# Values products of two key blocks back to back, query and key halves staged for three products, and a new order table, in an MLP, attention, MLP kernel

## The chip, the cores and the metric

One Trainium2 chip, one core. The metric is the device time of one execution in microseconds. PE is the matrix engine, PEld its weight load, ACT the scalar engine, DVE the vector engine, POOL GpSimd, SP the queue that starts transfers.

## The reference

Four sequences of 2048 rows of 256 numbers. Three residual layers follow one another: half an MLP, attention, half an MLP.

```python
x = x + 0.5 * ffn(layernorm(x));  x = x + attn(layernorm(x));  x = x + 0.5 * ffn(layernorm(x))
# ffn: input, hidden and weights rounded in blocks of 16 to a scaled grid of 8 magnitudes
h = silu(xq @ wgate_q.T) * (xq @ wup_q.T); y = quant(h) @ wdown_q.T          # 256 -> 704 -> 256
# attn: 8 heads, each a difference of two softmaxes over queries and keys of 16 numbers
q, k = rotary(rmsnorm(x @ Wq.T)), rotary(rmsnorm(x @ Wk.T)); v = x @ Wv.T    # 16 maps of 16, 8 values of 32
a = softmax(causal(q @ k.T / 4)); out = (a[first] - lam * a[second]) @ v
y = (layernorm(out) * (1 - LAMBDA_INIT)) @ Wproj.T
```

## The kernel before

The rows are cut into 64 tiles of 128; four tiles are a chunk, four chunks a sequence, so there are 16 chunks. A chunk goes through the first MLP (pass 0), the projections of attention (pass 1), attention itself, the output projection (pass 2) and the second MLP (pass 3). Different chunks are in different stages at a time, and the five engines each run one fixed list of work, joined by semaphores.

Attention goes in steps (`attention_steps`, L108): a step is one chunk of 512 queries, one group `g` of two heads (four score maps) and one block of 128 keys. There are 640 steps. A chunk with number 0, 1, 2, 3 in its sequence has 4, 8, 12, 16 key blocks for each of the four groups; in the last four blocks, on the diagonal, only 512, 384, 256 or 128 queries are left. A step is:

- `scores` twice (`u` 0 and 1, L1541 to L1553): PE multiplies a stack of key parts and a stack of query parts, 64 rows each, two products side by side in two halves of the array (its tiling is 64x128), into `psum_s0` or `psum_s1`. `scores(s, u)` waits until `exp(s-1, u)` has read that tile.
- `exp` twice (L1243): ACT reads a `psum_s` tile, 1024 numbers a row, and writes `probs`, a ring of three steps.
- `mask` (L1152): POOL, on diagonal blocks only.
- `values` (L1556 to L1571): PE multiplies four float32 probabilities with v, in four column strips (tiling 128x32), and adds them up in `psum_o`. The trace has each of the four float32 products as two instructions. It waits for its own step's exp or mask.

All other products on PE (`hidden` L1514, `down` L1527, `project_qk` and `project_v` L1538, `transpose_o` L1578, `project_out` L1588) use the whole array, 128x128, and are called fills here. So PE changes its tiling between scores, values and fills.

Queries and keys are kept as the float16 part and the float16 rest. `high_qk` (ACT, L1233) writes the float16 part of a tile twice into the four slots of `st_q` and of `st_k`, and `low_qk` (POOL, L1134 to L1143) writes the rest, float32 minus float16 part, twice, in one instruction for queries and one for keys. Slots are query: part, part, rest, rest; key: part, rest, part, rest; so a score is the sum of four products of halves. `turn_qk` (SP, L1062) turns both stacks by transposing transfers.

The order of each engine's list is made at build time. `whole_plan` (L253) adds stages with an engine, a weight from `COST` (L89), a due time and what they need, take and free; `Plan.order` (L161) then places one stage after another, the one that can start first, and among equals the one due first. Due times come from the table `DUE` (L61): spans, offsets and shifts for the chunks, and one nudge for each kind of stage. `SWITCH` (L105) is what the planner counts for a change of tiling.

Of the kernel before, what the change touches and what calls it, by code (L numbers as in the profile page):

```python
# [14 lines left out]
P = 128  # L15
# [40 lines left out]
EARLY = BATCHES * NCH  # L56

DUE = dict(lead=12, spans=(21, 703, 35, 11832, 953, 6799, 105, 2598, 104, 4129, 21, 1789, 27, 50, 55, 14564), tail=566708347155116, early=-0.41, mlp1=(149, 28), qkv=(41, 70), qk=(-35, 167), out=(-1336, 93), mlp2=(373, 152), shift=((-18, -8, -25, -3, 0), (-234, 83, 0, -6, 13), (-20, -9, -45, -17, 0), (-21, -3, -20, 2, 194), (13, 6, 1, 24, -5), (0, -15, -31, 3, 13), (-57, 0, 172, 14, 3), (-16, -29, -15, -10, 0), (59, 22, 6, 22, 13), (-6, -27, 4, -8, 1), (-10, -94, 16, 2, -6), (-3, 8, -3, -7, -16), (-12, -71, -111, 3, -54), (12, -3, -25, -41, -80), (-3, 10, 47, -15, -6), (21, 0, 0, 7, 0)),  # L61
           nudge=dict(add_down=-58, add_out=13, copy_xT=-55, dequant_h=35, dequant_x=-14,
                      divide_h=21, divide_x=1, down=3, gate=-26, grid_h=-3, grid_x=10, head_stats=4,
                      heads_out=-8, hidden=20, high_h=-6, high_x=11, load=-1, low_h=-2, low_qk=4,
                      low_x=-28, mask=-1, norm_a=149, norm_heads=-2, norm_qk=30, norm_x=52,
                      points_h=10, points_x=4, project_out=1, project_qk=-2, project_v=-2,
                      quant_h=6, quant_x=87, read_qk=-37, read_v=56, rms=45, rope=10, rope_add=-3,
                      scale_x=-10, scores=-517, stats=23, store=-7, tanh=5, transpose_o=15,
                      transpose_x=-26, turn_qk=13, turn_x=10, values=-6))
ST = 2  # L70
LANDING = 4.0
# [5 lines left out]

# [11 lines left out]
COST = dict(add_down=0.46, add_out=0.47, copy_o=0.67, dequant_h=1.38, dequant_x=1.06, divide_h=1.39,  # L89
            divide_x=1.06, down=1.97, gate=0.82, grid_h=0.89, grid_x=0.68, head_stats=2.75, heads_out=3.15,  # L90
            hidden=1.29, high_h=0.8, high_qk=1.16, high_x=0.64, low_h=1.52, low_qk=2.28, low_x=1.16,
            mask=0.63, norm_a=1.09, norm_heads=0.69, norm_qk=0.68, norm_x=0.78, points_h=0.89, points_x=0.69,
            project_out=0.69, project_qk=1.36, project_v=0.69, quant_h=1.65, quant_x=2.06, read_qk=0.69,
            read_v=0.48, rms=4.05, rope=1.93, rope_add=1.27, rstd=3.34, scale_x=1.29, square_h=0.79,
            square_x=0.62, stats=1.82, tanh=0.46, transpose_o=0.59)
OVERLAP = dict(tensor=0.0, vector=0.08, scalar=0.1, gpsimd=0.04, sync=0.0)
REACH = dict(tensor=0.14, vector=0.04, scalar=0.04, gpsimd=0.08, sync=0.1)
RELEASE = 0.06
DRAIN = 0.14
TILING = dict(scores=1, values=2)  # L100

PORT = dict(grid_h=0, points_h=0, norm_qk=0, norm_heads=0, norm_x=0, quant_x=0.81,
            divide_x=0, dequant_x=0, low_x=0, divide_h=0, dequant_h=0, low_h=0, rope_add=0, low_qk=0, mask=0)
PORT_LEAD = 0.14
SWITCH = 0.11  # L105
# [18 lines left out]
def by_act(key):  # L124

    pas, p = key
    return pas != 2 and 2 * p // NTC < EARLY


# [11 lines left out]
class Plan:  # L141

    def __init__(self, nudge):
        self.nudge = nudge
        self.stages = {}
        self.sizes = {}  # L150
        self.ring = {}
        self.bank = {}

    def add(self, name, engine, weight, due, needs=(), takes=(), frees=(), lands=0.0):
        weight = COST.get(name[0], weight)
        if engine == "tensor":
            lands += DRAIN
        self.stages[name] = (engine, weight, due + self.nudge.get(name[0], 0),
                             [n for n in needs if n], list(takes), list(frees), lands)

    def order(self):  # L161
        end, free_at = {}, dict.fromkeys(ENGINES, 0.0)
        freed = {r: {} for r in self.sizes}
        self.ring = {r: {} for r in self.sizes}
        banks = [[0.0, 0] for _ in range(BANKS)]
        out = {e: [] for e in ENGINES}
        tiling, left = 0, {}
        held = {"vector": 0.0, "gpsimd": 0.0, "part": 0.0}
# [7 lines left out]
        met = {name: 0.0 for name in self.stages if not missing[name]}  # L176
# [21 lines left out]
        while len(end) < len(self.stages):  # L198
            best = None
            for name in met:  # L200
                at = ready(name)
                if at is not None:
                    start = max(at, free_at[self.stages[name][0]])
                    if self.stages[name][0] == "tensor" and TILING.get(name[0], 0) != tiling:
                        start += SWITCH
                    if best is None or (round(start, 6), place[name]) < best[:2]:
                        best = (round(start, 6), place[name], start, name)
            assert best, "stages that wait for one another: " + str(list(met)[:20])
            start, name = best[2:]
# [9 lines left out]
            if name[0] in PORT and engine in held:  # L219
# [5 lines left out]
                extra = max(0.0, until - start - PORT_LEAD)  # L225
                held[engine] = start + extra + lock
                if engine == "gpsimd":
                    held["part"] = start + extra + (lock / 2 if name[0] == "low_qk" else lock)
# [17 lines left out]
        self.end = end  # L246
        return out
# [5 lines left out]
def whole_plan():  # L253
# [3 lines left out]
    plan = Plan(DUE["nudge"])  # L257
# [6 lines left out]
    def fill(name, weight, due, needs, takes=(), frees=()):  # L264

        add(name, "tensor", weight, due, needs, [("bank", name), *takes], frees)

    def halved(pas, p, due, made):

        u = ("x", pas, p)  # L270
        add(("high_x", *u), "scalar", .65, due, [made], [(rings_of(pas)[1], (pas, p))])
        add(("low_x", *u), "gpsimd", 1.35, due + .7, [("high_x", *u)], [], [(rings_of(pas)[0], (pas, p))])
        add(("turn_x", *u), "sync", .2, due + 2, [("low_x", *u)], [(rings_of(pas)[2], (pas, p))], [(rings_of(pas)[1], (pas, p))],
            lands=3.3)

    def quantise(kind, key, due, needs, takes, frees, times):

        quant, divide, square, grid, points, dequant, high, low, lands = times
        own, half, turned = (("xu", "x16", "xT16") if kind == "x" else ("hu", "h16", "hT16"))
        u = (kind, *key)  # L280
        q = ("quant_" + kind, *u)
        if kind == "x" and by_act(key):
            norm, q = ("norm_a", *u), ("scale_x", *u)
            add(norm, "scalar", .8, due, needs, takes, frees)
            add(q, "vector", 1.3, due, [norm], [("bank", q)], [("bank", q)])
        else:
            add(q, "vector", quant, due, needs, [*takes, ("bank", q)], [*frees, ("bank", q)])
        add(("divide_" + kind, *u), "gpsimd", divide, due + .1, [q])
        sq = ("square_" + kind, *u)
        place = ("gu", u) if kind == "h" else ("bank", sq)  # L290
        add(sq, "scalar", square, due + .2, [("divide_" + kind, *u)], [place])
        add(("grid_" + kind, *u), "vector", grid, due + .3, [("square_" + kind, *u)])
        add(("points_" + kind, *u), "vector", points, due + .4, [("grid_" + kind, *u)], [],
            [place] if kind == "x" else [])
        add(("dequant_" + kind, *u), "gpsimd", dequant, due + .5, [("points_" + kind, *u)], [], [place] if kind == "h" else [])
        add(("high_" + kind, *u), "scalar", high, due + .6, [("dequant_" + kind, *u)], [(half, key)])
        add(("low_" + kind, *u), "gpsimd", low, due + .7, [("high_" + kind, *u)], [], [(own, key)])
        add(("turn_" + kind, *u), "sync", .2, due + .8, [("low_" + kind, *u)], [(turned, key)], [(half, key)],
            lands=lands)

    def mlp(pas, tiles, due, pace, stats):
        for i in range(0, NTC, 2):
            d = due + pace * i
            pair = (pas, tiles[i] // 2)
            quantise("x", pair, d, [("rstd", *stats)], [("xu", pair)], [("stats", stats)] if i else [],
                     (2.3, 1.1, .7, .75, .75, 1.1, .65, 1.35, 3.3))
            for t in tiles[i:i + 2]:
                key = (pas, t)
                dt = d + 6 + pace * (t % 2)
                for part in range(len(PARTS)):  # L310
                    h = ("hidden", pas, t, part)
                    d1 = dt + 2 * part
                    fill(h, 1.3, d1, [("turn_x", "x", *pair), ("hidden", pas, t, part - 1) if part else
                                      ("hidden", pas, t - 1, len(PARTS) - 1) if t % 2 else None], [("hu", key)],
                         [("xT16", pair)] if part == len(PARTS) - 1 and t % 2 else [])
                    add(("tanh", *h), "scalar", .42, d1 + 1.6, [h])
                    add(("gate", *h[1:]), "vector", .9, d1 + 2, [("tanh", *h)], [], [("bank", h)])
                quantise("h", key, dt + 7, [("gate", pas, t, part) for part in range(len(PARTS))], [], [],
                         (1.6, 1.45, .85, 1.0, 1.0, 1.45, .8, 1.75, 4.2))
                dn = ("down", pas, t)  # L320
                fill(dn, 2.1, dt + 13, [("turn_h", "h", *key)], [], [("hT16", key)])
# [11 lines left out]
    for c in chunks:  # L333
        at.append(at[-1] + due["spans"][c])
# [1288 lines left out]
```

## Time and profile before

| what | value |
|---|---|
| runs | 2249.22, 2256.57 and 2260.17 us, median 2256.57 |
| the profiled execution, span from first to last instruction | 2257.2 us |
| its busy time | PE 1906.5, ACT 1724.0, DVE 1677.2, POOL 1438.6 us |
| its mean granted PE clock | 0.962 of full speed |

The page gives the profiled execution's span and no other time of it; the span is 0.6 us above the median of the runs. Busy times are sums over the execution and the engines work side by side, so none of them adds up to the span.

### The profile page before, as it was taken

How to read it: one execution, taken by the hardware profiler on the slowest of the kernel's cores; microseconds unless marked ns; L12 is line 12 of the kernel's file. 1: busy time of each engine (PE TensorE's matmuls, PEld its weight loads, DVE VectorE, ACT ScalarE, POOL GpSimd, SP SyncE). 2: the span in 40 equal slices, each digit the busy share in tenths (PEclk: the TensorE clock that was granted, in tenths of full speed). 3: DMA queues.
4: the chain of work that ended last, by engine and by line, in shares of the span. 5: the costliest groups of instructions: out<-in, count | busy, mean ns of one | idle time of the engine just before them, and what ended most of it. 6: DMA issues, size and time to landing. Idle time of an engine off the chain costs nothing. (4 is left out here: it accounts for less than half of the span.)

```text
span 2257.2 us, 39699 instructions
## 1 busy us (share of the span) xinstructions
PE 1906.5 (84%) x13634; PEld 776.0 (34%) x13634; DVE 1677.2 (74%) x3657; ACT 1724.0 (76%) x2598; POOL 1438.6 (64%) x1490
## 2 busy tenths in 40 slices
PE   2577889989989888999989888998998899988845
PEld 1233333333423333343333332343332433432312
DVE  8898988778837897878856897878864978834324
ACT  3446888878887887878888888887888799788842
POOL 3778886767735787766845786667763868723213
PEclk9789999999999999999999999999999999999977
DMA  4134444235212444233412334233231434211102
GB/s 110 27 64 85 72 76 76 50 62 89 42 45 38 71 71 90 59 54 76 75 45 38 73 67 88 45 75 61 52 63 40 81 63 86 52 39 20 35 10 45
DMA packets 477494, 136.19 MB, mean 60 GB/s; under 512 B 458222, under 2 KB 477038, under 8 KB 477294
## 3 DMA queue, kind: packets, MB, share of 16 engines
q1 hardware_dynamic: 477294, 133.65, 31.6%
q8 instruction: 110, 1.80, 0.3%
q14 instruction: 90, 0.74, 0.1%
HBM read 11.96 MB, written 8.39 MB: 9 GB/s over the span
## 5 line engine op out<-in xcount | busy, mean ns | idle before, releaser
L1243 ACT ACTIVATE probs<-psum_s 128x1024 f32<-128x1024 f32 (+3 forms) x1280 | 1072.9, 902 | 109.8 <-PE psum_s L1553 97.9
L1571 PE MATMUL psum_o<-probs,v_sb 128*32 128x512 f32 (+3 forms) x5120 | 581.8, 542 | 27.6 <-POOL probs L1152 14.7
L1514 PE MATMUL shared<-w_gu_T,xT 128*128 128x480 f16 (+1 forms) x2304 | 510.1, 369 | 84.6 <-DMA xT<-x 49.2
L1553 PE MATMUL psum_s<-q_stack,k_stack 64*128 64x512 f16 (+3 forms) x2560 | 390.8, 353 | 101.2 <-ACT probs L1243 91.6
L1514 PEld LDWEIGHTS shared<-w_gu_T,xT 128*128 128x128 f16 x2304 | 212.4, 99 | 371.6 <-issue 102.1
L1527 PE MATMUL shared<-w_down_T,hT 128*128 128x256 f16 x2176 | 272.7, 282 | 36.1 <-DMA hT<-h 16.4
L1166 ACT ACTIVATE hq<-shared,tanh_scale 128x240 f32<-128x240 f32 (+1 forms) x384 | 172.2, 458 | 133.1 <-PE shared L1514 128.2
L1152 POOL TENSOR_SCALAR_AFFINE_SELECT probs<-probs 128x512 f32<-128x512 f32 x256 | 181.3, 715 | 141.3 <-ACT probs L1243 140.0
L1553 PEld LDWEIGHTS psum_s<-q_stack,k_stack 64*128 64x128 f16 x2560 | 94.9, 93 | 508.3 <-ACT probs L1243 409.9
L1120 POOL TENSOR_TENSOR hq<-grid,qscale 128x704 f32<-128x704 f32 x128 | 182.6, 1428 | 112.6 <-DVE grid L1367 112.6
L1083 POOL TENSOR_TENSOR hq<-hq,rscale 128x704 f32<-128x704 f32 x128 | 186.1, 1455 | 104.0 <-DVE rscale L1277 103.8
L1527 PEld LDWEIGHTS shared<-w_down_T,hT 128*128 128x128 f16 x2176 | 210.9, 101 | 109.0 <-issue 35.5
L1127 POOL TENSOR_TENSOR h<-hq,h 128x704 f16<-128x704 f32 x128 | 201.9, 1578 | 63.3 <-ACT h L1204 63.3
L1127 POOL TENSOR_TENSOR x<-xq,x 128x512 f16<-128x512 f32 x128 | 158.6, 1243 | 95.8 <-ACT x L1204 95.7
L1571 PEld LDWEIGHTS psum_o<-probs,v_sb 128*32 128x32 f32 x5120 | 111.4, 108 | 268.1 <-issue 164.2
L1362 DVE SCALAR_TENSOR_TENSOR hq<-grid,hq 128x704 f32<-128x704 f32 x128 | 149.7, 1170 | 58.5 <-ACT grid L1177 58.1
L1348 DVE SCALAR_TENSOR_TENSOR hq<-hq,shared 128x240 f32<-128x240 f32 (+1 forms) x384 | 147.0, 383 | 58.7 <-ACT hq L1166 57.8
L1538 PE MATMUL shared<-w_qkv_T,xT 128*128 128x512 f16 (+1 forms) x768 | 146.0, 338 | 26.3 <-DVE xb L1374 6.2
L1367 DVE SCALAR_TENSOR_TENSOR grid<-grid,hq 128x704 f32<-128x704 f32 x128 | 160.9, 1257 | 3.3
L1350 DVE SCALAR_TENSOR_TENSOR hq<-hq,shared 128x240 f32<-128x240 f32 (+1 forms) x384 | 153.0, 398 | 13.2
L1190 ACT ACTIVATE xq<-xb,offset,rstd 128x256 f32<-128x256 f32 x192 | 103.5, 599 | 49.9 <-POOL offset L1111 40.6
L1177 ACT ACTIVATE grid<-hq 128x704 f32<-128x704 f32 x128 | 102.0, 797 | 47.4 <-POOL hq L1083 47.2
(133 smaller groups left out, 2372.8 us busy)
## 6 DMA issues: line engine op xcount, KB each, us to landing
xb<-L_attn_x SPq DMA_DIRECT2D x16, 512.0 KB, 4.1
out<-xb SPq DMA_DIRECT2D x16, 512.0 KB, 2.9
xT<-x SPq DMA_TRANSPOSE x128, 3.1
hT<-h SPq DMA_TRANSPOSE x128, 3.5
k_stack<-st_k SPq DMA_TRANSPOSE x64, 3.3
q_stack<-st_q SPq DMA_TRANSPOSE x64, 3.3
k_stack<-L_ffn_w_down SPq DMA_DIRECT2D x1, 704.0 KB, 4.2
k_stack<-L_ffn_w_gate SPq DMA_DIRECT2D x1, 480.0 KB, 6.0
```

Source lines behind the costliest of these rows:

```text
L1083: nc.gpsimd.tensor_tensor(by_block(a), by_block(a), rscale[:, i, 0:nb].unsqueeze(2).broadcast_to([P, nb, QB]), ALU.mult).then_inc(scaled_r ...
L1120: nc.gpsimd.tensor_tensor(by_block(a), by_block(g), qscale[:, i, 0:nb].unsqueeze(2).broadcast_to([P, nb, QB]), ALU.mult).then_inc(quantise ...
L1127: nc.gpsimd.tensor_tensor(low, buffers(kind, key)[0], high, ALU.subtract)\
L1152: nc.gpsimd.affine_select(out=blk, in_=blk, compare_op=ALU.is_ge, fill=0.0, base=0, pattern=[[0, 4], [1, P]], channel_multiplier=-1)\
L1166: nc.scalar.activation(buffers("h", h[1:3])[0][:, lo:hi], bank(h)[:, 0:hi - lo], ACT.Tanh, scale=tanh_scale[:, 0:1]).then_inc(tanh_done, 1)
L1243: nc.scalar.activation(probs[:, s % 3, 2 * u:2 * u + 2, q0:CHUNK], psum_s[u][:, :, q0:CHUNK], ACT.Exp, scale=HD ** -0.5 / QK_SCALE ** 2).t ...
L1350: nc.vector.scalar_tensor_tensor(h2, h2, H_SCALE, bank(h)[:, n:2 * n], ALU.mult, ALU.mult)\
L1367: nc.vector.scalar_tensor_tensor(points(e[1], e[2:]), g, GRID_BASE, a, ALU.add, ALU.subtract)\
L1514: last = nc.tensor.matmul(bank(e)[:, 0:2 * (hi - lo)], xs[:, x, t % 2, k, :], w_gu_T[:, w, k, 2 * lo:2 * hi], start=n == 0, stop=n == len( ...
L1527: last = nc.tensor.matmul(bank(e)[:, 0:C], hs[0:n, k, :], w_down_T[0:n, w, :], start=i == 0, stop=i == len(parts) - 1)
L1553: last = nc.tensor.matmul(psum_s[u][:, j, q0:CHUNK], k_stack[half, at, h, kt % NTC * P:(kt % NTC + 1) * P], q_stack[half, c % 2, h, q0:CHU ...
L1571: last = nc.tensor.matmul(psum_o[at:at + VD, q0:CHUNK], v_sb[:, kt // NTC % SLOTS * NTC + kt % NTC, 2 * g + u, :], probs[:, s % 3, 2 * u + ...
```

## The change

1. **Values in pairs.** In the plan, the values stage of an even key block `k` also needs the exp (or mask) of the next block. The two values stages of a pair can then follow each other on PE. The instructions and their semaphore waits are as before; only their places in PE's list change.
2. **Three products of halves.** One buffer `st` takes the place of `st_q` and `st_k`. Slots are query: part, part, rest, zero; key: rest, part, part, zero. `low_qk` becomes one instruction for queries and keys together that writes 512 numbers a row, where there were two of 512. The fourth slot is zeroed once at the start. The product of the two rests is left out. Score products, transfers and `high_qk` keep their sizes.
3. **Order.** `DUE` becomes a table of due times of each kind of stage, pass (or head group) and chunk, first and last, in integer nanoseconds; `LANDING` and `COST` are the same figures in nanoseconds, but `low_qk` is 1160 where it was 2.28 us. Paths that no stage took (`quant_x`, `norm_x`) are removed. The mask's semaphore count follows POOL's own order.

```diff
-DUE = dict(lead=12, spans=(21, 703, 35, 11832, 953, 6799, 105, 2598, 104, 4129, 21, 1789, 27, 50, 55, 14564), ...
+DUE = {
+    "add_down0": (94794, 240540, 58015, 44956, 84367, 91045, 158882, 108668, 804012, 943216, ...
...
+    def add(self, name, engine, at, needs=(), takes=(), frees=(), lands=0, weight=None):
+
+        family, c, i, n = at
+        first, last = DUE[family][2 * c:2 * c + 2]
+        weight = COST[name[0]] if weight is None else weight
...
-            add(("values", s), "tensor", .90 * w, d, [("mask", s) if diag is not None else ("exp", s, 1),
-                                                      ("values", s - 1) if s else None, ("read_v", tiles[-1])],
-                [("psum_o", (c, g))], [("probs", s)])
+            paired = s + (k + 1) % 2
+            add(("values", s), "tensor", at("values"), [("mask", s) if diag is not None else ("exp", s, 1),
+                                                        ("mask", paired) if steps[paired][5] is not None else ("exp", paired, 1),
+                                                        ("values", s - 1) if s else None, ("read_v", tiles[-1])],
+                [("psum_o", (c, g))], [("probs", s)], weight=900 * full // CHUNK)
...
-        st_q = sb("st_q", [P, ST, 2 * NH, 4, HD], F16)
-        st_k = sb("st_k", [P, ST, 2 * NH, 4, HD], F16)
+        st = sb("st", [P, ST, 2, 2 * NH, 4, HD], F16)
...
+                    nc.gpsimd.memset(st[:, :, :, :, 3, :], 0.0).then_inc(fills_done, 1)
...
-                            for j, (stage, hi, lo) in enumerate(((st_q, slice(0, 2), slice(2, 4)),
-                                                              (st_k, slice(0, 4, 2), slice(1, 4, 2)))):
-                                pool.wait_ge(hi_ready, 2 * t + j + 1)
-                                st = stage[:, t % ST]
-                                src = roped[:, t % NTC, j * C:(j + 1) * C].rearrange("p (h d) -> p h d", d=HD)
-                                nc.gpsimd.tensor_tensor(st[:, :, lo, :],
-                                                        src.unsqueeze(2).broadcast_to([P, 2 * NH, 2, HD]),
-                                                        st[:, :, hi, :], ALU.subtract).then_inc(lo_ready, 1)
+                            pool.wait_ge(hi_ready, 2 * t + 2)
...
+                            src = roped[:, t % NTC, :].rearrange("p (j h d) -> p j h d", j=2, d=HD)
+                            nc.gpsimd.tensor_tensor(parts(2 * HD, n - 2 * HD), src, parts(HD, n), ALU.subtract)\
+                                .then_inc(lo_ready, 1)
...
-                                pe.wait_ge(masked, d + 1)
+                                pe.wait_ge(masked, MASK["mask", s] + 1)
```

What the new order does is not seen in the table. Three places show it.

**PE in the middle**, around step 277 of 640 (the eighth chunk), where fills stand between attention steps. L1553 or L1585 are scores, L1571 or L1603 values, the others fills. Before:

```order
L1553 MATMUL psum_s<-q_stack,k_stack 128x512 x4
L1571 MATMUL psum_o<-probs,v_sb 32x512 x4
L1514 MATMUL shared<-w_gu_T,xT 128x480 x12
L1514 MATMUL shared<-w_gu_T,xT 128x448 x6
L1553 MATMUL psum_s<-q_stack,k_stack 128x512 x4
L1571 MATMUL psum_o<-probs,v_sb 32x512 x4
L1514 MATMUL shared<-w_gu_T,xT 128x480 x6
```

Now:

```order
L1585 MATMUL psum_s<-q_stack,k_stack 128x512 x4
L1603 MATMUL psum_o<-probs,v_sb 32x512 x8
L1585 MATMUL psum_s<-q_stack,k_stack 128x512 x4
L1546 MATMUL shared<-w_gu_T,xT 128x480 x12
L1546 MATMUL shared<-w_gu_T,xT 128x448 x6
L1559 MATMUL shared<-w_down_T,hT 128x256 x17
L1585 MATMUL psum_s<-q_stack,k_stack 128x512 x4
L1603 MATMUL psum_o<-probs,v_sb 32x512 x8
```

The values of two steps stand together, and the fills between the scores of two steps.

**PE at the end**, in the last group of the last chunk, where no fill is left. The numbers 0 and 1 of `psum_s` are `u`. Before:

```order
L1553 MATMUL psum_s0<-q_stack,k_stack 128x512 x2
L1553 MATMUL psum_s1<-q_stack,k_stack 128x512 x2
L1571 MATMUL psum_o<-probs,v_sb 32x512 x4
L1553 MATMUL psum_s0<-q_stack,k_stack 128x512 x2
L1553 MATMUL psum_s1<-q_stack,k_stack 128x512 x2
L1571 MATMUL psum_o<-probs,v_sb 32x512 x4
```

Now:

```order
L1585 MATMUL psum_s0<-q_stack,k_stack 128x512 x2
L1585 MATMUL psum_s1<-q_stack,k_stack 128x512 x2
L1585 MATMUL psum_s0<-q_stack,k_stack 128x512 x2
L1585 MATMUL psum_s1<-q_stack,k_stack 128x512 x2
L1603 MATMUL psum_o<-probs,v_sb 32x512 x8
```

Before, one step's values stand between the scores of any two steps; now nothing, and then the values of two.

**POOL**, the first tiles of queries and keys (`st`, `st_q` and `st_k` are the staged halves, `x`, `xq` and `hq` belong to other stages). Before:

```order
L1143 TENSOR_TENSOR st_q<-roped,st_q 128x16x32
L1143 TENSOR_TENSOR st_k<-roped,st_k 128x32x16
L1143 TENSOR_TENSOR st_q<-roped,st_q 128x16x32
L1143 TENSOR_TENSOR st_k<-roped,st_k 128x32x16
L1120 TENSOR_TENSOR xq<-xq,qscale 128x512
```

Now:

```order
L1192 TENSOR_TENSOR x<-xq,x 128x512
L1210 TENSOR_TENSOR st<-roped,st 128x2x16x16 x2
L1192 TENSOR_TENSOR x<-xq,x 128x512
L1152 TENSOR_TENSOR hq<-hq,rscale 128x704 x2
L1210 TENSOR_TENSOR st<-roped,st 128x2x16x16
```

Each tile has one instruction where it had two.

## Rows read from the trace of the kernel before

**Rows 1.** The page, part 1: busy time of each engine.

```profile
PE 1906.5 (84%) x13634; PEld 776.0 (34%) x13634; DVE 1677.2 (74%) x3657; ACT 1724.0 (76%) x2598; POOL 1438.6 (64%) x1490
```

**Rows 2.** Busy time by stretch: PE, PEld, DVE, ACT, POOL, granted clock, DMA share, GB/s.

```profile
200.00:2000.00 1800.00, 1617.53 (x11815) 654.37 (x11815) 1405.34 (x3087) 1476.46 (x2227) 1234.13 (x1269) 0.98 0.35 64
2000.00:2150.00 150.00, 131.81 (x1004) 40.59 (x1006) 55.38 (x126) 131.81 (x164) 39.72 (x44) 1.00 0.11 25
2150.00:2257.00 107.00, 50.70 (x280) 22.32 (x272) 42.43 (x93) 30.79 (x48) 32.07 (x32) 0.70 0.14 29
```

**Rows 3.** Waits of the whole span: engine, line waited for, total us, times, longest.

```profile
ACT probs L1243 <- PE psum_s L1553: 97.9, 125, 4.8
...
PE psum_s L1553 <- ACT probs L1243: 91.6, 179, 1.6
...
PE psum_o L1571 <- POOL probs L1152: 14.7, 30, 1.0
```

**Rows 4.** PE in order of time among fills: start us, length us, then the group.

```profile
829.85 1.39 PE L1514 MATMUL shared<-w_gu_T,xT 128*128 128x480 f16 x6
831.07 1.15 PE L1527 MATMUL shared<-w_down_T,hT 128*128 128x256 f16 x9
...
997.05 1.07 PE L1571 MATMUL psum_o<-probs,v_sb 128*32 128x512 f32 x8
998.05 1.39 PE L1514 MATMUL shared<-w_gu_T,xT 128*128 128x480 f16 x6
999.37 0.61 PE L1553 MATMUL psum_s<-q_stack,k_stack 64*128 64x512 f16 x4
999.90 1.06 PE L1571 MATMUL psum_o<-probs,v_sb 128*32 128x512 f32 x8
```

**Rows 5.** The same for PE, three values steps in a row.

```profile
2105.35 0.39 PE L1553 MATMUL psum_s<-q_stack,k_stack 64*128 64x512 f16 x2 [0.61 <-ACT probs L1243]
2105.67 0.66 PE L1578 MATMUL shared<-ident,o_sb 128*128 128x128 f32 x4
...
2106.58 2.78 PE L1571 MATMUL psum_o<-probs,v_sb 128*32 128x512 f32 x24
2109.30 0.60 PE L1553 MATMUL psum_s<-q_stack,k_stack 64*128 64x512 f16 x4
```

**Rows 6.** The same for PE in the attention-only end.

```profile
2138.41 1.92 PE L1571 MATMUL psum_o<-probs,v_sb 128*32 128x512 f32 x16
2140.27 0.61 PE L1553 MATMUL psum_s<-q_stack,k_stack 64*128 64x512 f16 x4
...
2142.16 1.07 PE L1571 MATMUL psum_o<-probs,v_sb 128*32 128x512 f32 x8
...
2147.79 1.06 PE L1571 MATMUL psum_o<-probs,v_sb 128*32 128x512 f32 x8
```

**Rows 7.** ACT in order of time in the same end.

```profile
2122.78 10.53 ACT L1243 ACTIVATE probs<-psum_s 128x1024 f32<-128x1024 f32 x12 [0.63 <-PE psum_s L1553]
...
2140.76 9.55 ACT L1243 ACTIVATE probs<-psum_s 128x1024 f32<-128x1024 f32 x10 [0.89 <-PE psum_s L1553]
```

**Rows 8.** Groups of POOL, shapes apart: count, busy us, mean ns, idle before.

```profile
L1143 POOL TENSOR_TENSOR st_k<-roped,st_k 128x512 f16<-128x512 f32 x64 | 82.4, 1288 | 0.0
L1143 POOL TENSOR_TENSOR st_q<-roped,st_q 128x512 f16<-128x512 f32 x64 | 81.9, 1279 | 39.6 <-ACT st_q L1233 39.5
...
L697 POOL TENSOR_TENSOR k_stack<-k_stack,hq 128x1536 f32<-128x1536 f32 x3 | 10.2, 3391 | 26.4 <-DVE k_stack L761 26.4
...
L691 POOL MEMSET v_sb<- 128x5120 f32 x1 | 4.4, 4370 | 0.0
```

**Rows 9.** Groups of DVE, shapes apart.

```profile
L1367 DVE SCALAR_TENSOR_TENSOR grid<-grid,hq 128x704 f32<-128x704 f32 x128 | 160.9, 1257 | 3.3
...
L1424 DVE TENSOR_TENSOR roped<-roped,qk_rstd 128x512 f32<-128x512 f32 x64 | 62.2, 1001 | 0.3
...
L1391 DVE TENSOR_TENSOR roped<-shared,rope_sb 128x512 f32<-128x512 f32 x64 | 43.5, 680 | 0.0
```

More of the change, by code:

```diff
@@ L54 @@
 XB = XC * NTC
[L56 to L69, printed above, removed]
@@ L224, in order @@
                     until = held["vector"]
[L225 removed]
+                extra = max(0, until - start - PORT_LEAD)
                 held[engine] = start + extra + lock
                 if engine == "gpsimd":
[L228 removed]
+                    held["part"] = start + extra + (lock // 2 if name[0] == "low_qk" else lock)
                 weight += extra
@@ L246, in order @@
         self.end = end
+        self.left = left
         return out
@@ L296, in quantise @@
[L296 to L301, printed above, removed]
+        add(("dequant_" + kind, *u), "gpsimd", at("dequant_" + kind), [("points_" + kind, *u)], [], [place] if kind == "h" else [])
@@ L307, in mlp @@
             for t in tiles[i:i + 2]:
                 key = (pas, t)
-                dt = d + 6 + pace * (t % 2)
                 for part in range(len(PARTS)):
                     h = ("hidden", pas, t, part)
-                    d1 = dt + 2 * part
-                    fill(h, 1.3, d1, [("turn_x", "x", *pair), ("hidden", pas, t, part - 1) if part else
-                                      ("hidden", pas, t - 1, len(PARTS) - 1) if t % 2 else None], [("hu", key)],
+                    at = lambda stage: (stage + str(pas), t // NTC, t % NTC * 3 + part, 3 * NTC - 1)
@@ L315, in mlp @@
+                    fill(h, at("hidden"), [("turn_x", "x", *pair), ("hidden", pas, t, part - 1) if part else
+                                           ("hidden", pas, t - 1, len(PARTS) - 1) if t % 2 else None], [("hu", key)],
                          [("xT16", pair)] if part == len(PARTS) - 1 and t % 2 else [])
[L316 to L319, printed above, removed]
+                    add(("tanh", *h), "scalar", at("tanh"), [h])
@@ L392, in whole_plan @@
         mine = steps_of(steps, c)
-        k = (span(c + 2) - span(c + 1)) / sum(CHUNK - steps[s][4] for s in mine)
-        d = span(c + 1)
         for s in mine:
             _, g, kt, is_last, q0, diag = steps[s]
-            w = (CHUNK - q0) / CHUNK
+            full = CHUNK - q0
+            k = kt - first_key(c)
+            at = lambda stage: (stage + str(g), c, k, NTC * (c % NCH + 1) - 1)
             for u in range(2):
                 before = s - 1 + u, 1 - u
-                add(("scores", s, u), "tensor", .23 * w, d + u * .1,
+                add(("scores", s, u), "tensor", at("scores"),
```

335 lines of the change are left out of this document (162 added, 173 removed), and 68 rows, old and new, of the table DUE.

## The prediction

> **What bounds the kernel now.** I read the busy times first, then the same by stretch, then the waits, then PE and ACT in order of time. PE has most of the work: 1906.5 of 2257.2 us [rows 1]. In the long middle, 200 to 2000 us, PE is busy 1617.5 of 1800 us, ACT 1476.5, DVE 1405.3, POOL 1234.1 [rows 2]. No engine is full, PE is the fullest. Of the end, 2000 to 2150 us, PE and ACT have 131.8 of 150 each, and DVE and POOL little [rows 2]: there attention is nearly alone, and the two hand the score tiles to each other. The last 107 us hold the last chunk's MLP, one stage after another. The waits say the same: PE waited 91.6 us for exps before scores and ACT 97.9 us for scores before exps [rows 3]. So the middle has PE as its tightest engine, with slack for one wait in ten, and the attention-only stretches are set by exp: from one values step at 2142.16 to the third after it at 2147.79 there are 1.88 us a step [rows 6], and ten exps take 9.55 us without a pause [rows 7].
>
> **Changes of tiling, the first term.** Values among other work, followed by a fill, hold PE 1.00 us (997.05 to 998.05) [rows 4]. Three in a row take 2.72 us (2106.58 to 2109.30) [rows 5]; less one of 1.00 that is 0.86 for each of the first two. Leaving values thus costs 0.14 us. Scores of one `u` take 0.32 us when something else follows (2105.35 to 2105.67) [rows 5]; both take 0.53 (999.37 to 999.90), so one costs 0.21 within the pair and leaving scores 0.11 [rows 4, 5]. A fill of six products lasts 1.22 us before another fill (829.85 to 831.07) and 1.32 before scores (998.05 to 999.37) [rows 4]: 0.10. Counted in the two orders, PE changes its tiling 1502 times before and 1242 times now: values are left 483 and 320 times, scores 672 and 588, fills 347 and 334. At 0.12 us for values (a little under the one reading, which rests on a single run of three) and 0.10 for the others: 163 x 0.12 + 97 x 0.10 = 29 us less work on PE. It counts in full only where PE sets the pace; its bounds are 0 (all of it before waits) and 260 x 0.14 = 36. I take 29, since PE is the fullest engine of the middle.
>
> That a change of tiling costs time at all is also in the Trainium skill (TensorEngine Tiling (Array Packing), Key Properties): changing the mode drains the array. The page gives no price; TensorE: Matmul & The Clock Gate (Step-by-step: what each phase is for) puts a drain at about 128 cycles, as an estimate 53 ns at 2.4 GHz and 14 us for 260 changes, with which the sum would come to 2241. The rows show twice that price.
>
> **The pause of a pair, the second term.** In the attention-only end PE now issues both scores of two steps and then two values steps. `scores(s, 0)` behind them comes late, and ACT runs out of tiles. The trace has this where two values steps happen to stand together: at 2138.41 they take until 2140.27 [rows 6], and ACT is idle 0.89 us before 2140.76; another such place costs ACT 0.63 us [rows 7]. By the rows: ACT has two exps, 2 x 0.95 = 1.9 us. In that time PE must do 0.32 of the second scores, 0.86 and 1.00 of values, and then the next scores, whose results ACT took up 0.49 us after they began (2140.27 to 2140.76) [rows 6, 7]: 2.67 us. That is 0.8 us a pair, so I take 0.9 from the nearer place. The pause counts only where neither engine has anything else. In the new order 144 of the 320 pairs have no other ACT work between the exps on their two sides; in the old one 51 values runs stood so, and their pauses are in its time. Of the 93 more, most have a fill of over a microsecond near, during which ACT catches up. Pairs with nothing but attention from one values pair to the next, on both engines, are 30 in the new order, 17 of them in the last chunk; a third are short diagonal steps or follow a fill. I charge 20 x 0.9 = 18 us; bounds 0 and 93 x 0.9 = 84.
>
> **The fuller mix.** By the same count the old order had 39 such attention-only pairs of steps. In one, PE has about 2 x (0.53 + 1.00) = 3.1 us to do in 2 x 1.88 [rows 4, 6], so 0.7 us idle. Nine fewer give 6 us. Bounds 0 and 12.
>
> **Waits before values.** PE stood 14.7 us before values because of masks [rows 3]. The first of a pair now comes after the second step's scores, and the second behind 0.86 us of the first's, so most masks are done. With the few waits for exps I take 10 us; bounds 0 and 20. What is queued behind a waiting values step is PE's whole list, the scores for ACT among it; that is the pause above.
>
> **POOL.** 64 instructions of 1.28 us go (of 128) [rows 8]: 82 us of 1438.6. POOL is not full, so its time itself is worth nothing; what it costs others is on DVE. A DVE product of 512 numbers from two tiles in SBUF takes 1001 ns and one with an input in PSUM 680 [rows 9]. Scaled to 704, 680 would be 935 where `grid` has 1257. Over 64 and 128 instructions that is 21 + 41 = 62 us held up, and 82/1438.6 of it is 3.5: I take 4, bounds 0 and 10. The latency of staging (1.28 us a tile) is hidden by the steps of the chunk before. The one more fill at the start writes 1024 half-size numbers, where one of 5120 takes 4.37 us; POOL then waits 26.4 us for DVE anyway [rows 8], so it costs nothing; without that cover under 1 us. The score products keep 64 rows, so the dropped product saves PE nothing.
>
> **Start and tail.** Before the first scores PE has one `hidden` more, behind the last values the same four output projections, twelve `hidden` and four `down`. So neither moves the time.
>
> **Sum.** 2257.2 - 29 - 6 - 10 - 4 = 2208.2; with 18 for the pauses 2226.2. The profiled execution lies 0.6 us above the median, so I keep **2226**.
>
> **Rivals.**
> - *The pauses decide (slower).* Time = 2208 + 0.9 for each pair whose pause lies on the path. At 54 pairs the gain is gone, at 67 it is slower by 0.5%, with all 93 it is 2292. For it: PE and ACT are 90% and 82% busy in the middle [rows 2], so a pause has little to hide in, and fills now stand in larger blocks. Against: at most 30 pairs are attention alone. Chance 0.15.
> - *Switches were never on the path (no change).* Where PE waits 91.6 us for exps [rows 3], a change of tiling sits in front of a wait, and the other engines take over. With a quarter of the gains and no pauses charged: 2257 - 12 = 2245; with some pauses 2250. Chance 0.17.
> - *The new order packs better than my counts.* PE is idle 182 + 18 us between 200 and 2150 [rows 2]. If the finer table removes a further fifth, 40 us: 2186. Nothing in the trace can show it; the counts by place show much the same mix. Chance 0.18.
> - That the change does not do what it says I can exclude: all 320 pairs stand together in PE's list.
>
> **Chances.** Forecast 0.50, better packing 0.18: faster by over 0.5% (about what a measurement of this kernel can tell from no change) 0.68. Same 0.17, slower 0.15. The range, 2190 to 2268, takes the forecast's bounds, the unchanged case and the first part of the slower one; it leaves out the far half of the better packing and pauses at over 67 pairs.
>
> **What would show it.** PE's values followed by values 0.86 to 0.88 us, by others 1.00; PE busy near 1880; POOL near 1357, with one `st` instruction of 1.28 us for each tile; DVE's 1001 ns a little lower; ACT idle 0.6 to 0.9 us at each pair after 2070 us, and 25 us more idle in attention-only stretches. Wrong if ACT's wait for scores rises from 97.9 by over 50 us while PE's wait for exps does not fall, or if the time lost or won lies in the start, the tail or waits for transfers.

## The result, and the profile after

The change makes the kernel slower: 2275.28 us (median of 4 runs, 2274.22 to 2277.04) against 2255.15 us before on the same chip. The ratio is 1.009, 95% interval 1.0071 to 1.0108. The forecast was 2226 us, with a range of 2190 to 2268.

The page of the changed kernel, parts 1 and 5 (busy us and mean ns, then the idle time of the engine before the group and what ended it):

```profile
PE 1885.3 (83%) x13634; PEld 801.9 (35%) x13634; DVE 1648.8 (72%) x3657; ACT 1726.7 (76%) x2598; POOL 1352.6 (59%) x1427
...
L1308 ACT ACTIVATE probs<-psum_s 128x1024 f32<-128x1024 f32 (+3 forms) x1280 | 1077.5, 900 | 155.0 <-PE psum_s L1585 122.7
...
L1603 PE MATMUL psum_o<-probs,v_sb 128*32 128x512 f32 (+3 forms) x5120 | 558.1, 554 | 5.4 <-POOL probs L1218 4.1
L1585 PE MATMUL psum_s<-q_stack,k_stack 64*128 64x512 f16 (+3 forms) x2560 | 392.5, 357 | 165.6 <-ACT probs L1308 156.2
```

Its busy time by stretch, as in [rows 2]:

```profile
200.00:2000.00 1800.00, 1594.18 (x11763) 673.66 (x11761) 1368.87 (x3070) 1474.41 (x2219) 1137.72 (x1198) 0.97 0.35 64
2000.00:2150.00 150.00, 125.99 (x967) 45.22 (x964) 59.30 (x132) 122.54 (x156) 48.43 (x51) 0.97 0.15 32
2150.00:2275.00 125.00, 62.00 (x380) 26.00 (x378) 45.95 (x101) 45.00 (x63) 32.01 (x33) 0.75 0.12 25
```

Its waits, as in [rows 3]:

```profile
PE psum_s L1585 <- ACT probs L1308: 156.2, 251, 5.9
...
ACT probs L1308 <- PE psum_s L1585: 122.7, 180, 3.2
...
ACT probs L1308 <- PE psum_o L1603: 29.8, 46, 2.7
...
PE psum_o L1603 <- POOL probs L1218: 4.1, 7, 1.5
```

and of the kernel before, the same wait of ACT and the page's line of the values:

```profile
ACT probs L1243 <- PE psum_o L1571: 8.2, 10, 2.4
...
L1571 PE MATMUL psum_o<-probs,v_sb 128*32 128x512 f32 (+3 forms) x5120 | 581.8, 542 | 27.6 <-POOL probs L1152 14.7
```

PE's work fell as planned, 1906.5 to 1885.3 us. PE's idle time before values is nearly gone (5.4 us where it was 27.6, and the masks' part is 4.1 where it was 14.7). But PE waits 156.2 us for exps before scores, where it waited 91.6; ACT waits 122.7 us for scores, where it waited 97.9, and 29.8 us for values to free a probability tile, where it waited 8.2. Both engines wait for each other more. In the middle all four engines are less busy than in [rows 2]; for PE and POOL a part of that was planned.

By place, in the two profiled executions: the first scores start at 219.9 us where they started at 215.1, the last values at 2185.5 where it was 2165.4, and behind them 89.8 us are left where 91.8 were. So of 18.1 us, 15.1 lie between the first scores and the last values, 4.8 before and -2.0 behind.

PE in order of time in the last group of attention of the changed kernel (start, length, group; the last line is the pair on the diagonal):

```profile
2154.37 1.93 PE L1603 MATMUL psum_o<-probs,v_sb 128*32 128x512 f32 x16
2156.23 0.61 PE L1585 MATMUL psum_s<-q_stack,k_stack 64*128 64x512 f16 x4
2157.80 0.39 PE L1585 MATMUL psum_s<-q_stack,k_stack 64*128 64x512 f16 x2 [0.96 <-ACT probs L1308]
2158.71 0.39 PE L1585 MATMUL psum_s<-q_stack,k_stack 64*128 64x512 f16 x2 [0.53 <-ACT probs L1308]
...
2182.19 1.71 PE L1603 MATMUL psum_o<-probs,v_sb 128*32 128x512 f32 x16
```

and ACT there:

```profile
2156.72 3.77 ACT L1308 ACTIVATE probs<-psum_s 128x1024 f32<-128x1024 f32 x4 [0.89 <-PE psum_s L1585]
2161.38 3.77 ACT L1308 ACTIVATE probs<-psum_s 128x1024 f32<-128x1024 f32 x4 [0.89 <-PE psum_s L1585]
2166.04 3.77 ACT L1308 ACTIVATE probs<-psum_s 128x1024 f32<-128x1024 f32 x4 [0.89 <-PE psum_s L1585]
2170.70 3.77 ACT L1308 ACTIVATE probs<-psum_s 128x1024 f32<-128x1024 f32 x4 [0.89 <-PE psum_s L1585]
```

This is the pause of a pair, five times alike (the fifth, from 2175.37, is not printed): PE works on two values steps from 2154.37 to 2156.23, ACT is idle 0.89 us before 2156.72, does four exps in 3.77 us and is idle 0.89 us again. A pair of steps lasts 4.66 us (2156.72 to 2161.38), where two steps lasted 2 x 1.88 [rows 6]. PE in turn waits 0.96 and 0.53 us for exps.

Not all of the longer waits are of this kind. The longest wait of PE for an exp is 5.9 us, where it was 1.6 [rows 3]. PE and ACT around it:

```profile
1174.81 0.50 PE L1585 MATMUL psum_s<-q_stack,k_stack 64*128 64x384 f16 x4
1181.19 0.39 PE L1585 MATMUL psum_s<-q_stack,k_stack 64*128 64x256 f16 x2 [5.88 <-ACT probs L1308]
...
1182.59 3.21 PE L1603 MATMUL psum_o<-probs,v_sb 128*32 128x512 f32 x16
```

```profile
1178.37 2.08 ACT L1256 ACTIVATE xq<-xb,offset,rstd 128x256 f32<-128x256 f32 x4 [3.96 <-POOL offset L1178]
```

ACT's list has a layernorm in front of the exps, and ACT stood 3.96 us for POOL's part of it. That comes from the new order, not from a pair.

These lines show the clock too. The granted clock was 1.00 of full speed from 1170 to 1175 us, and 0.50 (1.2 GHz, the lower of its two levels) from 1180 to 1185, behind this idle time. At that level the two values steps of a pair on the diagonal take 3.21 us, where at full clock they take 1.71 (2182.19). The mean granted clock is 0.955, where it was 0.962. Added up over all stretches at 0.50, PE was busy for 98.7 us in the kernel before and for 130.4 in the changed one. If work takes twice as long at 0.50, half of that is what the clock cost: 49 and 65 us, an estimate. So 16 us of PE's busy time came back by the clock, and at an equal clock its work would have fallen by some 37 us, not 21. How much of the 16 lies on the path isn't known; no run holds the clock fixed.

### The profile page after: what moved, and what is told of

Read it like the earlier page. It is cut to its first block and busy times, and to the rows that moved or that the text cites. A ratio compares the mean times of both kernels' runs of the same rounds, so it can differ in the third digit from the quotient of the medians.

```text
span 2275.3 us, 39703 instructions
## 1 busy us (share of the span) xinstructions
PE 1885.3 (83%) x13634; PEld 801.9 (35%) x13634; DVE 1648.8 (72%) x3657; ACT 1726.7 (76%) x2598; POOL 1352.6 (59%) x1427
## 5 line engine op out<-in xcount | busy, mean ns | idle before, releaser
L1308 ACT ACTIVATE probs<-psum_s 128x1024 f32<-128x1024 f32 (+3 forms) x1280 | 1077.5, 900 | 155.0 <-PE psum_s L1585 122.7
L1603 PE MATMUL psum_o<-probs,v_sb 128*32 128x512 f32 (+3 forms) x5120 | 558.1, 554 | 5.4 <-POOL probs L1218 4.1
L1585 PE MATMUL psum_s<-q_stack,k_stack 64*128 64x512 f16 (+3 forms) x2560 | 392.5, 357 | 165.6 <-ACT probs L1308 156.2
L1585 PEld LDWEIGHTS psum_s<-q_stack,k_stack 64*128 64x128 f16 x2560 | 98.2, 94 | 552.0 <-ACT probs L1308 446.1
L1185 POOL TENSOR_TENSOR hq<-grid,qscale 128x704 f32<-128x704 f32 x128 | 181.1, 1415 | 122.7 <-DVE grid L1399 122.7
L1603 PEld LDWEIGHTS psum_o<-probs,v_sb 128*32 128x32 f32 x5120 | 136.0, 111 | 277.1 <-issue 237.5
L1394 DVE SCALAR_TENSOR_TENSOR hq<-grid,hq 128x704 f32<-128x704 f32 x128 | 138.1, 1079 | 54.1 <-ACT grid L1243 53.5
L1406 DVE SCALAR_TENSOR_TENSOR xb<-shared,down_scale,xb 128x256 f32<-128x256 f32 x128 | 59.6, 467 | 113.9 <-PE shared L1559 113.5
```

The lines of the kernel that those rows point to most:

```text
L1185: nc.gpsimd.tensor_tensor(by_block(a), by_block(g), qscale[:, i, 0:nb].unsqueeze(2).broadcast_to([P, nb, QB]), ALU.mult).then_inc(quantise ...
L1308: nc.scalar.activation(probs[:, s % 3, 2 * u:2 * u + 2, q0:CHUNK], psum_s[u][:, :, q0:CHUNK], ACT.Exp, scale=HD ** -0.5 / QK_SCALE ** 2).t ...
L1585: last = nc.tensor.matmul(psum_s[u][:, j, q0:CHUNK], k_stack[half, at, h, kt % NTC * P:(kt % NTC + 1) * P], q_stack[half, c % 2, h, q0:CHU ...
L1603: last = nc.tensor.matmul(psum_o[at:at + VD, q0:CHUNK], v_sb[:, kt // NTC % SLOTS * NTC + kt % NTC, 2 * g + u, :], probs[:, s % 3, 2 * u + ...
```

## The experiments

Times are ratios to the kernel before, run on the same chip, with their intervals; 0.1% is 2.3 us. The difference of two such ratios is uncertain by some 0.2 to 0.3%, or 5 to 7 us.

### One part of the change alone: three products

```diff
-        st_q = sb("st_q", [P, ST, 2 * NH, 4, HD], F16)
-        st_k = sb("st_k", [P, ST, 2 * NH, 4, HD], F16)
+        st = sb("st", [P, ST, 2, 2 * NH, 4, HD], F16)
```

with `high_qk`, `low_qk`, `turn_qk` and the zeroed slots of the change, on the lists of the kernel before.

> The kernel before, its order list for list, with the three products of halves alone (one staging instruction of 1.28 us a tile on POOL for two). All theories want POOL 82 us less busy. If POOL costs others only by holding up DVE (62 us before): 2 to 10 us faster, DVE's L1424 product under 1001 ns. If staging were on the way to the scores: 20 us or more faster. If the change's loss came from the staging (a slower instruction with two strides): slower by 5 us or more, and the instruction well over 1.28 us.

Ratio 0.9935 (0.9913 to 0.9956), 2238.85 us: 15 us faster, the fastest of all kernels here, and under both kernels of the case. Its page, part 1, and the groups of the staging instruction and of the DVE product:

```profile
PE 1899.6 (85%) x13634; PEld 773.7 (35%) x13634; DVE 1658.1 (74%) x3657; ACT 1721.5 (77%) x2598; POOL 1355.2 (61%) x1427
```

```profile
L1146 POOL TENSOR_TENSOR st<-roped,st 128x512 f16<-128x512 f32 x64 | 78.8, 1234 | 59.2 <-ACT st L1234 53.0 <-DVE roped L1425 6.0
...
L1425 DVE TENSOR_TENSOR roped<-roped,qk_rstd 128x512 f32<-128x512 f32 x64 | 53.9, 872 | 0.3
```

POOL has 83 us less, DVE 19 us less, and the DVE product of 1001 ns takes 872. The gain is four times what I gave it, and lies between the two theories' numbers.

### Where that gain comes from

```diff
+                            for again in range(2):
+                                if t or again:
+                                    pool.wait_ge(unused_set, 2 * t + again)
+                                nc.gpsimd.memset(st[:, t % ST, :, :, 3, :], 0.0).then_inc(unused_set, 1)
```

> Three products alone gained 15 us where 4 were forecast. Here POOL gets the time back in another form: two fills of the zero slots (some 0.5 us each, written only, no input read) in front of each tile's staging instruction, 64 tiles. If the gain came from POOL's time and the length of the staging chain: most of it goes, ratio 0.997 to 1.000. If it came from DVE no longer held up by an instruction with inputs in SBUF: it stays, ratio 0.993 to 0.995, and DVE's product L1425 stays near 872 ns.

Ratio 0.9973 (0.9959 to 0.9987). Its groups:

```profile
L1150 POOL MEMSET st<- 128x512 f16 x128 | 67.0, 524 | 53.6 <-DVE roped L1430 22.8 <-issue 22.8 <-ACT st L1239 4.1
...
L1430 DVE TENSOR_TENSOR roped<-roped,qk_rstd 128x512 f32<-128x512 f32 x64 | 51.1, 828 | 0.3
```

The fills take 67 us of POOL, and its busy time is up by 60 (1414.7 where it was 1355.2). The DVE product stayed short (828 ns), and DVE's busy time too (1660.3), yet about three fifths of the gain went, 9 of 15 us with some 6 of uncertainty. So POOL's time and the length of the staging stage are a large part of the 15 us, by the medians the larger one. What is left may be DVE no longer held up, or the part of POOL's time that wasn't given back. Which of POOL's two, its occupation or the staging's length on the way to the scores, isn't told apart.

### Pairing alone, at the end and everywhere

```diff
+def together(pe, first, last):
+    out = list(pe)
+    for k in range(first, last, 2):
+        e = ("values", k)
+        out.remove(e)
+        out.insert(out.index(("values", k + 1)), e)
+    return out
...
+            order["tensor"] = together(order["tensor"], 608, 636)
```

> The kernel before, with the values of steps 608 to 635 in pairs, ten pairs that were not together before, at the end where attention is alone. Theory of the pause: ACT idle 0.89 us at each new pair, last values 8 to 9 us later, the whole run 8 to 9 us slower. Theory of switches (PE's work decides): 18 changes of tiling fewer, 2 us faster.

Ratio 1.0033 (1.0019 to 1.0047): 7 us slower for ten pairs, 0.7 us each, a little under the 0.89 of the pause.

> The kernel before with 306 of 320 pairs put together by moving the first values step down to the second, nothing else moved, and the old table: pairing alone. Changes of tiling 1502 to 1251, values runs with no other ACT work beside them 51 to 125. Theory of the pause: 0.9 us for each of the 74 more that lies on the path, less 28 us of switches: 2250 to 2295, slower than before by 10 to 40 us, with PE's wait for exps before scores up by 60 us or more. Theory of switches: 25 us faster. Theory that the new table costs what the change lost: within 5 us of before.

Ratio 1.029 (1.0266 to 1.0314), 2319.11 us: 65 us slower, more than any theory had. Its waits:

```profile
PE psum_s L1569 <- ACT probs L1259: 185.9, 300, 2.1
...
ACT probs L1259 <- PE psum_s L1569: 132.3, 174, 3.9
...
ACT probs L1259 <- PE psum_o L1587: 41.2, 68, 2.0
```

They are those of the changed kernel, stronger: PE's wait for exps doubled against 91.6, ACT's for a free probability tile is 41.2 where it was 8.2. Pairing alone makes waits of the kind that the change has. Its longest wait of PE is 2.1 us, so pairs alone don't make the 5.9 of the changed kernel. The mean granted clock is 0.955 here too.

### The change without its pairs

In three runs the first values step of a pair moves up in front of the second step's scores; the rest of the changed lists stays. The first of them does so from step 608 on, the second where ACT has only exps around the pair, the third everywhere.

```diff
+    for k in range(0, sum(e[0] == "values" for e in pe), 2):
+        i = out.index(("values", k))
...
+        j = i
+        while out[j - 1][0] == "scores" and out[j - 1][1] > k + 1:
+            j -= 1
...
+                out.insert(j, out.pop(i))
```

> The changed kernel with the first values step of each pair moved up in front of the second step's scores from step 608 on only, where attention is alone. Theory of the pause: 13 pairs lose 0.89 us each, less their 27 changes of tiling that ACT's pace hides: last values 9 to 12 us earlier, 2263 to 2267. Theory that PE's work decides: 27 changes more, 3 us slower, 2278.

Ratio 1.0069 (1.0056 to 1.0082) against the change's 1.009: 2269.39 us, 6 us faster. ACT in order of time at the end:

```profile
2152.12 22.36 ACT L1326 ACTIVATE probs<-psum_s 128x1024 f32<-128x1024 f32 x24 [0.62 <-PE psum_s L1603]
2175.22 1.08 ACT L1326 ACTIVATE probs<-psum_s 128x512 f32<-128x512 f32 x2 [0.73 <-PE psum_s L1603]
```

24 exps in 22.36 us without a pause; the changed kernel has one after every four. So the pause is shown. The last values start 7.0 us earlier (2178.4 against 2185.5), which is 0.5 us for each of the 13 pairs where I expected 0.7 to 0.9.

> The changed kernel, in which the first values step of a pair moves up in front of the second step's scores wherever ACT has nothing but exps around the pair; runs of values without other ACT work 144 to 9, changes of tiling 1242 to 1409. Theory of the pause: the pauses of 0.89 us go, 20 to 45 us faster than the change: 2230 to 2255, at or below the kernel before. Theory of switches: 167 more changes at 0.11 us, 15 to 18 us slower than the change. Theory of the table: within 5 us of the change, 2275.

Ratio 1.0157 (1.0134 to 1.018): 14 us slower than the change. Here the pause theory failed as I had stated it. That ACT has only exps around a pair doesn't mean that taking the pair apart wins anything. The loss is that of 167 more changes of tiling at 0.1 us, but the waits say that this isn't all: ACT waits 156.9 us for scores, where the change has 122.7, and PE waits 151.6 for exps, about as before (156.2).

> The changed kernel with the first values step of all pairs moved up over the second step's scores where nothing else stands between. 342 changes of tiling more than the change. By switches at 0.1 us: 34 us slower, ratio 1.024. If the pairs' pauses were the change's loss: faster than the change (ratio under 1.009). If the changed lists are fitted to pairs: 40 to 80 us slower, ratio 1.027 to 1.045.

Ratio 1.0373 (1.035 to 1.0396): 63 us slower than the change, as the theory of lists fitted to pairs had it; 34 us of it would be 342 changes of tiling at 0.1 us.

### Lists made anew

The changed kernel without the need that pairs (one line):

```diff
-                                                        ("mask", paired) if steps[paired][5] is not None else ("exp", paired, 1),
```

> The changed kernel without the one need that pairs the values, lists made anew from the new table: new table and three products, no pairs. If pairing is what costs and the table is sound: 2205 to 2240, at or under the kernel before with three products alone (2239). If the table was fitted to pairs and is worth nothing without them: 2255 to 2300. If pairing itself costs nothing: 2275.

Ratio 1.0385 (1.0367 to 1.0403).

The other way round, old table with three products (`low_qk=1.16` in `COST`), with and without that need:

> The kernel before with three products and the pairing need, lists made anew from the old table: the change without its refitted table. Pairs cost 65 us on the old lists and three products gained 15. If the new table won back what pairing cost: 2295 to 2320. If making the lists anew is enough: 2275, as the change. If the pairs gain by their switches once POOL is relieved: under 2240.

Ratio 1.0367 (1.0346 to 1.0388).

> The kernel before with three products and the shorter weight of the staging stage in the planner, lists made anew from the old table, no pairs. It differs from the run with three products alone (2239) by the lists only. If the lists' fit matters little: within 10 us of 2239. If the lists are finely fitted, a replanning without a new fit loses: 2245 to 2280.

Ratio 1.0358 (1.0343 to 1.0372): 2334.73 us, 96 us more than the same instructions on the old lists (2238.85). Its page, part 1, and two waits:

```profile
PE 1934.4 (83%) x13634; PEld 784.6 (34%) x13634; DVE 1662.8 (71%) x3657; ACT 1726.7 (74%) x2598; POOL 1355.4 (58%) x1427
```

```profile
PE psum_s L1554 <- ACT probs L1244: 128.8, 234, 2.5
...
ACT probs L1244 <- PE psum_s L1554: 119.2, 136, 3.6
```

One weight changed in the planner, and the lists are worth 96 us less. A part of that is the clock: 0.949 on average, where the same instructions on the old lists had 0.964. All three replannings without a new fit come out at 2335 to 2341, with and without pairs, each slower than the slowest theory had it; among lists that fit nothing, the 5 us between pairs and none (2339 and 2335) are within the noise. So these three say how much a fit is worth (64 us for the new table on paired lists, 2339 to 2275), and nothing of pairing.

### Which pairs cost

Three products on the old lists (0.9935) as the base, and parts of the pairs alone, named in a list. Of the 320 pairs 103 already stand together there, and 14 can't be moved without a circle of waits. The waits of the base:

```profile
ACT probs L1244 <- PE psum_s L1554: 96.3, 126, 3.7
...
PE psum_s L1554 <- ACT probs L1244: 89.1, 172, 1.6
...
ACT probs L1244 <- PE psum_o L1572: 10.1, 13, 2.1
```

```diff
+    for k in PAIRED:
+        e = ("values", k)
+        out.remove(e)
+        out.insert(out.index(("values", k + 1)), e)
```

> The kernel before with three products (0.9935 of before), its lists as they are but for 27 values steps moved down to their partner's place over scores alone, where ACT has other work beside exps. 44 changes of tiling fewer. If a switch counts where ACT has something else to do: 3 to 5 us faster than the three products alone, ratio 0.992. If a pair delays the next scores whatever ACT has: 5 to 20 us slower, ratio 0.996 to 1.002.

These 27 have other ACT work beside them. Ratio 1.0035 (1.0022 to 1.0048): 22 us over the base for 27 pairs, 0.8 us each.

> The same base, with 132 values steps moved down over a fill that stood between the two. 135 changes of tiling fewer. By switches: 13 us faster, ratio 0.988. By the delay of the first values step (the ring of three probability tiles keeps exp waiting, two steps of values stand in front of the next scores): 20 to 45 us slower, ratio 1.002 to 1.014.

These 132 had a fill between the two values steps. Ratio 1.0022 (1.0011 to 1.0033): 20 us for 132 pairs, 0.15 us each. Its waits:

```profile
PE psum_s L1574 <- ACT probs L1264: 128.6, 235, 1.9
...
ACT probs L1264 <- PE psum_s L1574: 99.2, 139, 4.1
...
ACT probs L1264 <- PE psum_o L1592: 35.3, 59, 2.0
```

> The same base, with 44 values steps moved down over scores alone, where ACT has only exps around them. 72 changes of tiling fewer, values runs without other ACT work 51 to 90. By the pause of 0.9 us: 20 to 35 us slower, ratio 1.002 to 1.009. By switches: 7 us faster, ratio 0.990.

These 44 have only exps on ACT around them; nine of them are among the ten at the end that were paired above. Ratio 1.006 (1.0038 to 1.0082): 28 us for 44 pairs, 0.65 us each. Its waits:

```profile
PE psum_s L1570 <- ACT probs L1260: 126.7, 224, 1.6
ACT probs L1260 <- PE psum_s L1570: 125.9, 147, 3.9
```

The three parts add up to 70 us, about what all pairs cost together on the kernel before (65). Where two values steps were apart by scores alone, putting them together costs 0.65 to 0.8 us, nearly the 0.88 by which the next scores come later (the first values step of a pair takes that long until the second starts), and it is not less where ACT has other work. Nor does it hang on the end: if nine of the 44 cost 0.7 each as above, the other 35 cost 0.6. Where a fill stood between, it costs 0.15; there ACT's wait for scores hardly moves (99.2), and its wait for a free probability tile rises from 10.1 to 35.3 us. In the 44, it is ACT's wait for scores that rises, by 30 us. These prices are net of the changes of tiling that are saved, and they hold a share of the clock: its mean was 0.958, 0.959 and 0.960 in the three, and 0.964 in the base.

### The control: moves the other way

The same base, values steps moved up, out of runs.

> The kernel before with three products (0.9935), and 54 values steps moved up, in front of scores, out of runs of values that have only exps on ACT around them; runs without other ACT work 51 to 3, changes of tiling 1502 to 1574. If the pause of 0.9 us is what matters wherever ACT has only exps: 20 to 35 us faster, ratio 0.979 to 0.985, faster than all so far. If any move away from the fitted lists costs, whichever way it goes: 10 to 25 us slower, ratio 0.998 to 1.005. By switches alone: 7 us slower, ratio 0.997.

Ratio 0.9962 (0.9946 to 0.9978): 6 us over the base with 72 more changes of tiling, as by switches alone, and hardly clear of the noise.

> The same with 145 values steps moved up wherever only scores stand between, whatever ACT does. 194 changes of tiling more than with the fitted lists. Pause theory: about as the lone ones, less 20 us of switches, ratio 0.985 to 0.995. Fit theory: 30 to 60 us slower, ratio 1.007 to 1.02. By switches alone 20 us slower, ratio 1.002.

Ratio 1.0079 (1.0057 to 1.0101): 32 us over the base for 145 moves and 194 more changes of tiling, some 20 us of it at 0.1 us a change.

So a move costs about 0.1 to 0.2 us upwards and 0.65 to 0.8 downwards over scores. If any step away from the fitted lists were to blame, both ways would cost alike. So it is the pair, or the later values step that makes it; the two come together in every run. But the fitted lists had put pairs where they cost nothing: taking those apart gained nothing.

> Three products alone, with the values steps from 608 on that stood together moved apart (614, 622 and 624 stand in the end without fills). Pause theory: 0.6 to 0.9 us for each of the three or four, 2 to 3.5 us faster than the three products alone, ratio 0.992 to 0.993. Otherwise 0.9935 or more.

Ratio 0.9937 (0.9914 to 0.996): the base again. The gain of 2 to 3.5 us isn't seen, and would be too small to be told from nothing.

## Why the prediction was wrong

- **Changes of tiling: the size was about right, the worth was not.** The price holds roughly (the two values steps of a pair take 1.86 us, 2154.37 to 2156.23, where two alone take 2.00 [rows 4]), and PE's busy time fell by 21 us, or some 37 at an equal clock, against 29 forecast. But PE had the time to spare: its wait for exps grew by 65. "It counts in full only where PE sets the pace; I take 29, since PE is the fullest engine of the middle" was the wrong end of my bounds. Fullest at 90% is not the bound when two engines pass tiles to each other through two score tiles and three probability tiles.
- **The pause of a pair: the mechanism was right, the count failed.** I had 0.9 us, and it is 0.89. I charged 20 pairs, those with nothing but attention on both engines. On the old lists the runs charge nearly every pair that was made out of values with scores between: 71 such pairs cost 50 us, 27 of them where ACT had other work. The step that failed is "most have a fill of over a microsecond near, during which ACT catches up": 35 pairs away from the end, with only exps on ACT, cost 0.6 us each, and the 27 with other ACT work 0.8. The reason that I give is argued: the next scores come 0.88 us later wherever the pair stands, and ACT's own list is fixed, so its other work isn't there when the gap is. The ring of three probability tiles adds a second wait that I hadn't listed at all (8.2 to 29.8 us). On the changed kernel's own lists only the 13 pairs at the end are shown to cost (6 us); taking apart the others made it slower.
- **The fuller mix** (6 us) was argued from counts and is nowhere seen: between 200 and 2150 us ACT, whose work is the same, is busy 1597 us where it was 1608.
- **The clock had no term.** It took back an estimated 16 us of PE's busy time. The prediction took PE's busy time as work alone, though a part of it was slow work at the lower level.
- **Waits before values** (10 us): those for masks fell by 10.6 us and all idle before values by 22, and the time came back before the scores.
- **POOL: 4 us forecast, 15 measured.** I costed only DVE held up, and that too low: its busy time fell by 19 us, where I had 3.5. Lengthening POOL's list by fills, which leave DVE as it was, takes about three fifths of the gain away; so POOL's own time at 64% busy, or the staging stage's length, was not free.
- **Start and tail.** The tail moved by -2.0 us. The first scores start 4.8 us later, which I had at nothing; but with the old lists they start anywhere from 214.3 to 219.4 us in the profiles, against 219.9 here, so it isn't clear that the change made it.
- **The signs.** Those of the mechanism came: PE 1885 us busy, POOL 1353, ACT idle 0.88 or 0.89 us at pairs of full steps at the end. My sign of being wrong, over 50 us more wait of ACT for scores, did not (24.8 us more), so it was badly chosen: the time showed as PE's wait for exps.
- **The rival that held** is "the pauses decide" (chance 0.15), with its break-even at 54 pairs: 2208 + 0.9 n gives n = 75 for the measured time. That n is only solved for, not counted, and the 2208 under it is wrong in several terms. By the runs the sum reads: 2255, less 15 for three products, plus 65 for pairing on the old lists, makes 2305; the change has 2275, so the new table won back some 30. That last number is a difference of sums, not a run of its own: pairing and table can't be run apart, since lists that are not fitted lose 64 to 96 us whatever is in them. Nor is it all gain: the wait of 5.9 us above is the new order's own. Whether a longer fit would make pairs pay stays open.

## What to carry to other kernels

In this kernel two engines hand tiles to each other through a short ring, and there batching one engine's work to save its switches delays the next hand-over by one batch: price that delay (here 0.88 us) against the saving (here 0.2 us a pair) at every place, not only where nothing else runs. Look at the granted clock before crediting a fall in PE's busy time, since new idle time can take part of it back. When a change comes with a new order, run its other parts on the old lists first: here one part alone was 0.65% faster, and the rest had buried it. And a fitted order belongs to the exact weights that it was fitted with; it has to be kept as a list, or fitted again.

## What was not expected of the hardware

- The larger surprise was the schedule's. A POOL engine that was busy 64% of the time gave back 15 us of 82 when relieved, and DVE 19 us of its busy time with it (8 of them in a product with both inputs in SBUF, 1001 to 872 ns). With 67 us of fills on POOL, which read nothing, the product took 828 ns: they did not hold it up.
- The pause is sharp: 0.88 or 0.89 us at each of the eight pairs of full steps from 2130 to 2176 us of the changed kernel, and 0.83 where the next steps are short ones on the diagonal.
- Two kernels with the same instructions can differ in the granted clock by their order alone: 0.964 and 0.949 on average for three products on the fitted and on the replanned lists.
